# A new order of the instructions of one group in the semilinear stage, on TensorE, VectorE and ScalarE

## The reference, cut to what matters

```python
x = x + xattn(ctx, ctx, layernorm(x), ...)        # ends with "@ Wo.T + bo"
x = x + semilinear(layernorm(x), ...)             # the stage that changes
x = x + ffn(layernorm(x), gate_w, expert_w)       # expert = argmax of the scores

# semilinear: q, k, v = short_conv(h @ W), 4 taps along the tokens; lr = softplus(h @ Wlr + 0.001)
# the 32 tokens are 2 chunks of 16; per head (16 heads of 32) the state is W_in, W_out, 4 rows each
def step(carry, chunk):
    k_h = softmax(k . W_in) * lr;  q_h = softmax(q . W_in)
    qk = where(causal, q_h . k_h, 0)
    o = q_h @ W_out + qk @ v
    W_out = W_out + k_h.T @ v
    for _ in range(2):
        attn = softmax([W_in | W_out] . [k | v] * scale)     # over the tokens of the chunk
        G = attn @ [v | k]
        W_in, W_out = W_in + lr0 * G_in, W_out + lr1 * G_out
# output: o @ Wo, added to x
```

## Time and profile before

| | us |
|---|---|
| median of three runs | 1295.08 (1293.03 to 1295.43) |
| the profiled execution | 1292.32 |
| its span, first to last instruction | 1290.5 |
| TensorE busy in the span | 1073.4 (83%) |
| VectorE busy | 841.3 (65%) |
| ScalarE busy | 494.5 (38%) |
| GpSimd busy | 328.1 (25%) |
| first sk0 of group 0 | 533.95 |
| first sk0 of group 1, of group 7 | 599.66, 1047.99 |
| mean granted TensorE clock of the span | 0.905 of full |

### The profile page before, as it was taken

How to read it: one execution, slowest core, us unless ns; L and a number is a source line. 1 busy time by engine, 2 the same in 40 slices (tenths; PEclk the granted TensorE clock), 3 DMA queues, 4 the chain that set the end, 5 groups by cost and what they waited for, 6 DMA issues and landing times. The chain is left out here.

```text
span 1290.5 us, 18724 instructions
## 1 busy us (share of the span) xinstructions
PE 1073.4 (83%) x6268; PEld 795.1 (62%) x6268; DVE 841.3 (65%) x1611; ACT 494.5 (38%) x954; POOL 328.1 (25%) x297
## 2 busy tenths in 40 slices
PE   5993999999999836888898979888898966793997
PEld 4882656666666524676685857667585755673443
DVE  3664478778786843669687776968678694724332
ACT  1221366667775741334332423434242332420110
POOL 0345367757775620000000000000000000002453
PEclk9996989989999757989899989999899997775999
DMA  4372212102210002000101001010100020128441
GB/s 158 111 285 65 52 40 55 33 23 55 55 33 17 17 18 66 1 34 1 50 1 50 1 3 50 1 50 2 37 15 1 18 98 34 66 82 314 127 153 58
DMA packets 59925, 75.06 MB, mean 58 GB/s; under 512 B 37759, under 2 KB 42303, under 8 KB 57793
## 3 DMA queue, kind: packets, MB, share of 16 engines
q1 hardware_dynamic: 52384, 52.98, 13.0%
q0 software_dynamic: 5152, 12.59, 3.1%
q10 hardware_dynamic: 2304, 8.39, 1.6%
HBM read 56.65 MB, written 22.81 MB: 62 GB/s over the span
## 5 line engine op out<-in xcount | busy, mean ns | idle before, releaser
L1184 POOL COPY fw_hx<-fw_hT 128x128 f32<-128x128 f32 x32 | 8.0, 293 | 520.8 <-ACTq L1653 520.8
L544 POOL TENSOR_TENSOR aw_wtent<-aw_tent,aw_e 128x1760 f32<-128x1760 f32 x32 | 100.7, 3146 | 113.6 <-DVE aw_e L540 113.6
L733 PE MATMUL aw_psum_kv<-all_xWv,aw_c 128*128 128x512 f32 x256 | 124.4, 632 | 0.0
L516 POOL TENSOR_TENSOR aw_tent<-all_const,all_ix 128x1760 f32<-128x1760 f32 x32 | 100.6, 3146 | 5.1 <-POOL aw_wtent L544 4.6
L839 ACT ACTIVATE aw_cT<-aw_psum_av 32x256 f32<-32x256 f32 x128 | 80.6, 630 | 38.7 <-PE aw_psum_av L762 37.6
L721 PE MATMUL aw_psum_kv<-aw_c,all_xWk 128*128 128x352 f32 x256 | 81.2, 473 | 9.5 <-POOL aw_A L620 9.5
L1946 PE MATMUL ex_psum_y<-ex_We,ex_gT 128*128 x184 | 84.1, 602 | 0.0
L733 PEld LDWEIGHTS aw_psum_kv<-all_xWv,aw_c 128*128 128x128 f32 x256 | 49.2, 202 | 52.8 <-issue 51.0
L527 DVE TENSOR_TENSOR aw_prod<-aw_tent,aw_psum_s 128x1760 f32<-128x1760 f32 x32 | 63.5, 1984 | 23.3 <-ACT aw_tent L522 16.8
L1680 ACT ACTIVATE fw_at<-fw_at,fw_atop 128x128 f32<-128x128 f32 x128 | 49.5, 388 | 66.9 <-DVE fw_atop L1327 66.9
L743 PEld LDWEIGHTS aw_psum_s<-aw_K,aw_Qb 128*128 128x128 f32 x512 | 66.5, 208 | 6.8 <-issue 4.7
(11 more groups left out here) (258 smaller groups left out, 2251.4 us busy)
## 6 DMA issues: line engine op xcount, KB each, us to landing
ex_We<-expert SPq DMA_DIRECT2D x1, 8192.0 KB, 22.6
aw_craw<-ctx SPq DMA_DIRECT2D x8, 704.0 KB, 4.9
xh_scr<-fw_x SPq DMA_DIRECT2D x10, 512.0 KB, 3.7
pj_x<-x_tok SPq DMA_DIRECT2D x8, 512.0 KB, 3.9
q_scr<-pj_QT ACTq DMA_DIRECT2D x8, 512.0 KB, 2.9
aw_Qb<-q_scr SPq DMA_DIRECT2D x32, 128.0 KB, 3.5
c_scr<-aw_cT ACTq DMA_DIRECT2D x8, 512.0 KB, 2.7
fw_cT<-c_scr SPq DMA_DIRECT2D x8, 512.0 KB, 4.8
```

The costliest lines, as they stand in the source:

```text
L516: return nc.gpsimd.tensor_tensor(self.tent[r][:], bc(rows, 1, self.nu * NK), bc(ix, 2, self.wr), ALU.subtract)
L544: return eng.tensor_tensor(self.wtent[:], self.tent[r][:], bc(self.e[:].rearrange("p u k -> p (u k)"), 2, self.wr), ALU.mult)
L733: mm = nc.tensor.matmul(ps_kv[:, j % 2, :], rows, Wv[:, c, :], start=(c == 0), stop=(c == KC - 1))
```

## The change

The instructions of a group stay the same; their order changes on TensorE, VectorE and ScalarE, with both plans. TensorE's order per group becomes: y0 kt0 vt0 sk0 sq0 khT1 qhT1 y1 qk1 si0 o1 up z0 z1 so0 khT0 qhT0 t0 t1 qk0 q3 q1 q0 q2 ti0 to0 k0 gi0 vt1 go0 o0 si1 so1 k3 k1 lr v3 v2 ti1 v1 to1 gi1 go1 v0 k2 sk1 wo sq1. On VectorE the masks of qk1 stand ahead of the weights of chunk 0, `enter` is cut in two (`normal_rows` behind the update of W_out), the masks of qk0 stand behind the maxima of step 0, and convolutions stand singly or in pairs between the steps. On ScalarE the base copies stand in the same manner between the copies of ti, to, vt1, o0, and `rates_ln` behind the exponentials of chunk 1. `convolve` counts by the place in `CONV`, the plan's own order; `maxima` waits for both scores. The groups without a predecessor and the end are brought into the same order. Of the diff, the lines that are new or stay (those that go are in the functions above); indentation is cut:

```diff
+def normal_stats(nc, m, chain, x, stats, mv, var, tiles):
...
+def normal_rows(nc, chain, x, h, mv, rstd, std, tiles):
+
     chain.eng.wait_ge(std.sem, std.at(chain.i, 1))
     chain.link(nc.vector.reciprocal(rstd[:, 0:tiles], rstd[:, 0:tiles]))
...
+FRONT = [("y0", "dve"), ("y1", "dve"), ("t0", "act"), ("t1", "act"), ("q3", "dve"), ("q1", "dve"), ("q0", "dve"),
+         ("q2", "dve"), ("k0", "dve"), ("k3", "dve"), ("k1", "dve"), ("lr", "dve"), ("v3", "dve"), ("v2", "dve"),
+         ("v1", "dve"), ("v0", "dve"), ("k2", "dve")]
+CONV = [n for n, _ in FRONT if n[0] in "qkv"]
...
+BACK = [("kt0", "act"), ("vt0", "act"), ("sk0", "dve"), ("sq0", "dve"), ("khT1", "act"), ("qhT1", "act"),
+        ("qk10", "dve"), ("qk11", "dve"), ("qk12", "dve"), ("qk13", "dve"), ("si0", "dve"), ("o1", "act"),
+        ("up", "dve"), ("z0", "dve"), ("z1", "dve"), ("so0", "dve"), ("khT0", "act"), ("qhT0", "act"),
+        ("qk00", "dve"), ("qk01", "dve"), ("qk02", "dve"), ("qk03", "dve"), ("ti0", "act"), ("to0", "act"),
+        ("gi0", "dve"), ("vt1", "act"), ("go0", "dve"), ("o0", "act"), ("si1", "dve"), ("so1", "dve"),
+        ("ti1", "act"), ("to1", "act"), ("gi1", "dve"), ("go1", "dve"), ("sk1", "dve"), ("wo", "act"), ("sq1", "dve")]
...
# VectorE, group
     exponents(i, ch, 0)
     if has_prev:
         causal_products(i, 1)
     else:
+        back.skip_reads(dve, "dve", i, "qk10", "qk11", "qk12", "qk13")
+    dve.wait_ge(lr_done.sem, lr_done.at(i, 1))
+    weights(t, ch, 0)
+    masked(i, "si0", 0)
     if not last:
         enter(n)
+    add_own_heads(i, ch, "up", 0, wout0, wout).then_inc(w_done.sem, 1)
+    if not last:
+        entered(n)
     if has_prev:
         leave(t.prev(), i)
+    else:
+        back.skip_reads(dve, "dve", i, "z0", "z1")
     masked(i, "so0", 1)
     maxima(i, ch, 0)
     if last:
         gate_stats(0)
+    causal_products(i, 0)
     normalise(t, ch, 0)
+    ahead("q3", "q1", "q0")
     step_weights(i, ch, 0)
     if last:
         gate_rows(0)
+    ahead("q2")
     masked(i, "si1", 0)
+    ahead("k0")
     masked(i, "so1", 1)
     maxima(i, ch, 1)
+    if last:
+        gate_stats(1)
+    ahead("k3", "k1")
     if not last:
         rates_in(n)
     normalise(t, ch, 1)
+    ahead("v3")
     if not last:
         rates_add(n)
+    ahead("v2", "v1")
     step_weights(i, ch, 1)
     if last:
         gate_rows(1)
+    ahead("v0", "k2")
     exponents(i, ch, 1)
+    weights(t, ch, 1)
     if not last:
         rates_out(n)
     ch.close()
...
# TensorE, group
+    go("y0")
     pe.wait_ge(conv_done.sem, conv_done.at(i, 3 * KC))
+    transposes(i, back, "kt0", [key[:, g, halves[0]] for g in by_g])
+    transposes(i, back, "vt0", [v[:, g, halves[0]] for g in by_g])
     blocks(i, back, "sk0", KC, [(key[:, g, halves[0]], win0[:, g, :]) for g in by_g])
     blocks(i, back, "sq0", KC, [(q[:, g, halves[0]], win0[:, g, :]) for g in by_g])
+    if has_prev:
+        turned_softmax(t.prev(), i, 1)
+    else:
+        back.skip(pe, i, "khT1", "qhT1")
+    go("y1")
+    if has_prev:
+        causal(i, 1)
+    else:
+        back.skip(pe, i, "qk10", "qk11", "qk12", "qk13")
     blocks(i, back, "si0", KC, [(win0[:, g, :], key[:, g, halves[0]]) for g in by_g])
     if has_prev:
         output(t.prev(), i, 1)
     else:
+        back.skip(pe, i, "o1")
+    pe.wait_ge(p_done.sem, p_done.at(i, 1))
     pe.wait_ge(*back.used(i, "vt0"))
     blocks(i, back, "up", KC, [(vt[0][:, g, :], e[0][:, 0, g * P:(g + 1) * P]) for g in by_g])
+    if has_prev:
+        project(i, 0)
+        project(i, 1)
+    else:
+        back.skip(pe, i, "z0", "z1")
+    pe.wait_ge(w_done.sem, w_done.at(i, 1))
+    blocks(i, back, "so0", KC, [(wout[:, g, :], v[:, g, halves[0]]) for g in by_g])
+    turned_softmax(t, i, 0)
     go("t0", "t1")
     causal(i, 0)
+    go("q3", "q1", "q0", "q2")
+    pe.wait_ge(n_done.sem, n_done.at(i, 1))
+    transposes(i, back, "ti0", [at[:, 0, g, :] for g in by_g])
+    transposes(i, back, "to0", [at[:, 1, g, :] for g in by_g])
+    go("k0")
+    pe.wait_ge(*back.used(i, "ti0"))
+    blocks(i, back, "gi0", KC, [(vt[0][:, g, :], atT[:, 0, g, :]) for g in by_g])
+    transposes(i, back, "vt1", [v[:, g, halves[1]] for g in by_g])
+    pe.wait_ge(*back.used(i, "to0"))
+    blocks(i, back, "go0", KC, [(kt[:, g, :], atT[:, 1, g, :]) for g in by_g])
+    output(t, i, 0)
+    pe.wait_ge(w_done.sem, w_done.at(i, 2))
+    blocks(i, back, "si1", KC, [(win[:, g, :], key[:, g, halves[0]]) for g in by_g])
+    blocks(i, back, "so1", KC, [(wout[:, g, :], v[:, g, halves[0]]) for g in by_g])
+    if last:
+        gate_turn(0)
+        gate_score(0)
+        gate_turn(1)
+    go("k3", "k1", "lr", "v3", "v2")
+    pe.wait_ge(n_done.sem, n_done.at(i, 2))
+    transposes(i, back, "ti1", [at[:, 0, g, :] for g in by_g])
+    go("v1")
+    transposes(i, back, "to1", [at[:, 1, g, :] for g in by_g])
+    pe.wait_ge(*back.used(i, "ti1"))
+    blocks(i, back, "gi1", KC, [(vt[0][:, g, :], atT[:, 0, g, :]) for g in by_g])
+    pe.wait_ge(*back.used(i, "to1"))
+    blocks(i, back, "go1", KC, [(kt[:, g, :], atT[:, 1, g, :]) for g in by_g])
+    go("v0", "k2")
     if last:
         gate_score(1)
     pe.wait_ge(w_done.sem, w_done.at(i, 3))
     blocks(i, back, "sk1", KC, [(key[:, g, halves[1]], win[:, g, :]) for g in by_g])
+    transposes(i, back, "wo", [wout[:, g, :] for g in by_g])
     blocks(i, back, "sq1", KC, [(q[:, g, halves[1]], win[:, g, :]) for g in by_g])
...
# ScalarE, group
+    take(i, "kt0", kt[:])
     take(i, "vt0", vt[0][:])
+    if has_prev:
+        take(i, "khT1", khT[1][:])
+        take(i, "qhT1", qhT[1][:])
+    else:
+        back.skip_reads(act, "act", i, "khT1", "qhT1")
     exponentials(i, 0)
     if has_prev:
+        take(i, "o1", oT[:, :, P:2 * P])
     else:
+        back.skip_reads(act, "act", i, "o1")
+    if not last:
+        deviation(n)
     take(i, "khT0", khT[0][:])
     take(i, "qhT0", qhT[0][:])
     if not last:
         turned(n)
     row_exponentials(i, 0)
+    ahead("q3", "q1", "q0", "q2")
     take(i, "ti0", atT[:, 0])
+    ahead("k0")
     take(i, "to0", atT[:, 1])
     if last:
         gate_deviation(0)
+    take(i, "vt1", vt[1][:])
+    ahead("k3", "k1")
+    if last:
         gate_copy(0)
     row_exponentials(i, 1)
+    if last:
+        gate_copy(1)
     if not last:
         rates_exp(n)
+    ahead("v3")
+    take(i, "o0", oT[:, :, 0:P])
+    ahead("v2")
     take(i, "ti1", atT[:, 0])
+    ahead("v1")
     take(i, "to1", atT[:, 1])
+    if last:
+        gate_deviation(1)
+    ahead("v0", "k2")
+    take(i, "wo", wrow[:])
+    exponentials(i, 1)
     if not last:
         rates_ln(n)
```

More of the change, by code:

```diff
@@ L1145, in group @@
                 else:
-                    sp.wait_ge(*back.full(t.r, "sk0"))
+                    sp.wait_ge(*back.full(t.r, BACK[0][0]))
                     sp.wait_ge(x_out.sem, x_out.at(t.r - 1, 0))
@@ L1383, in group @@
                 exponents(i, ch, 0)
-                masked(i, "si0", 0)
-                dve.wait_ge(lr_done.sem, lr_done.at(i, 1))
-                weights(t, ch, 0)
                 if has_prev:
@@ L1420, in group @@
                     gate_rows(1)
-                ahead("v2", "v3")
+                ahead("v0", "k2")
                 exponents(i, ch, 1)
+                weights(t, ch, 1)
                 if not last:
                     rates_out(n)
-                weights(t, ch, 1)
                 ch.close()
             enter(FIRST)
-            convolve(FIRST, ["q0", "q1", "q2", "q3"])
+            entered(FIRST)
+            convolve(FIRST, CONV[:7])
             rates_in(FIRST)
             rates_add(FIRST)
-            convolve(FIRST, [f"{n}{e_}" for n in "kv" for e_ in range(KC)])
+            convolve(FIRST, CONV[7:])
             rates_out(FIRST)
@@ L1435, in _ @@
             rounds(dve, NG, group, 1)
-            back.skip_reads(dve, "dve", NG, *BEGIN)
+            back.skip_reads(dve, "dve", NG, "sk0", "sq0")
             gate_stats(2)
@@ L1439, in _ @@
             gate_rows(2)
+            back.skip_reads(dve, "dve", NG, "si0", "up")
             leave(LAST, NG)
@@ L1566, in group @@
-                transposes(i, back, "kt0", [key[:, g, halves[0]] for g in by_g])
-                go("y0", "y1")
+                if has_prev:
[7 more added lines that the diff above has]
+                    back.skip(pe, i, "qk10", "qk11", "qk12", "qk13")
                 blocks(i, back, "si0", KC, [(win0[:, g, :], key[:, g, halves[0]]) for g in by_g])
@@ L1611, in group @@
                 blocks(i, back, "sk1", KC, [(key[:, g, halves[1]], win[:, g, :]) for g in by_g])
+                transposes(i, back, "wo", [wout[:, g, :] for g in by_g])
                 blocks(i, back, "sq1", KC, [(q[:, g, halves[1]], win[:, g, :]) for g in by_g])
-                transposes(i, back, "vt1", [v[:, g, halves[1]] for g in by_g])
-                transposes(i, back, "wo", [wout[:, g, :] for g in by_g])
                 if last:
@@ L1623, in _ @@
             rounds(pe, NG, group, 1)
```

(20 more changed lines are left out.)

94 lines of the change are left out of this document (14 added, 80 removed), and 3 rows, old and new, of the table BACK.

## The result

The changed kernel takes 1239.8 us (median of four runs, 1232.5 to 1240.1) where the kernel before takes 1295.1 (1293.0 to 1295.4): ratio 0.956, 95% interval 0.953 to 0.960. Forecast: 1234, range 1220 to 1260. Run again on another occasion it took 1234.5 (1233.5 to 1237.5) against 1297.0, ratio 0.952 (0.950 to 0.953); this second base is the one for the experiments. These were run on three occasions, each with the kernel before beside it (1297.0, 1295.3 and 1296.5), so the ratios compare better than the medians.

What follows compares the result with a forecast made beforehand. TensorE, its waits and its slowed clock were taken to bound each 74.7 us group. Savings of 52.3 (six groups) + 4 + 5 = 61 from 1292.3 gave 1231, put at 1234 for the median; range 1220 to 1260.

Steps and rivals of the forecast that it cites:

- A group of 66.0 us: Groups 1 to 6 of the semilinear stage: each goes from 74.7 to 66.0 us, bounds 63.5 and 70.5.
- The replay: The new order worked through one steady group with profile durations: 64.7 us, 61.7 of work and 3.0 of waits.
- The branch, 0.85 on the mean: TensorE's wait at the loop's branch: adds 2.1 us in every second group, 0.45 filling an existing wait.
- The clock, 2.9 us per group: TensorE's o1 and following work, at the 1.2 GHz level behind a 2.67 us wait: 2.9 us lost per group.
- The table load: ScalarE's load of the exponential's table ahead of step 0, 1.28 us: covered by four q projections, priced at nothing.
- Group 0, 4 us: First group, with no chunk behind it: gain 4 us, bounds 0 and 6, with so0 waiting 5.7 us.
- Group 7, 5 us: Last group, without projections: kt0 to the step's transposes 37.9 us, step 0 saves another 1.6; gain 5, bounds 0 and 8.
- Behind it nothing changes: Claim that behind the last group, group 7, the time stays the same: no gain or loss.
- (a): Rival: waits come back in the steps behind base copies and convolutions; a group takes 70.5 to 71, total 1267; chance 0.12.
- (b): Rival: 63.5 to 64.5 us per group if the branch's wait falls into an existing one; 1222, down to 1216; chance 0.14.
- (c): Rival: TensorE's clock falls to 1.2 GHz during short pieces of work; a group takes 81 us, total 1330; chance 0.03.
- (d): Rival: VectorE's chain sets the 74.7 us group, so waits only move and nothing changes; 1295, chance 0.02.

Runs made afterwards that it cites:

- the weights first: Changed kernel with VectorE doing the softmax weights of chunk 0 ahead of the masks of chunk 1's causal products: 1258.0 us, ratio 0.969.
- matmuls of no use: Changed kernel with added 128x512 matmuls into a free PSUM bank where TensorE waits in the last group and gate's end: 1228.8 us, ratio 0.947.
- y1 in halves: Changed kernel with y1's eight matmuls issued in two halves, ahead of and behind the causal products of chunk 1: 1230.0 us, ratio 0.949.

## Why the prediction was right, point by point

**A group of 66.0 us: 66.46.** The replay gave 64.7 without the branch; the trace has 65.8, and without the loop 65.0. Its waits were 0.45, 0.9, 1.05, 0.3, 0.25; measured 0.65, 0.76, 0.78, 0.82, 0.24. Up's is the one that is far off: 0.82 in the loop, 0.40 without it, as VectorE has small pauses within the weights of chunk 0 that straight code lacks. The 0.45 added for hand-overs was too small by more than half for the 1.1 us that were missing, and its reason was mostly another: 0.8 of them go with the loop. The wait ahead of the turned softmax I had put down to the weights; the trace names the copy of vt0, which stands on ScalarE behind the logarithm's table load (601.85), moved there by the change. Both end within 0.1 us of each other (the weights at 604.33, the copy at 604.40), so taking one away alone would win 0.1 us at most. No run tries it.

**The branch, 0.85 on the mean: near, by luck.** I had a pause in every second group, three of six. The trace of the kernel before has two, which at the forecast's 1.65 us net would be 0.55 on the mean. In the changed kernel the two groups behind a branch take 3.1 and 1.6 us more than the other four, 0.8 on the mean, and 0.3 of that is a second cost that I missed, the fall of the clock behind one of the two (1.7 us). The kernel without a loop gains 1.5 us per group: this 0.8, and the 0.7 that every group has.

**The clock, 2.9 us per group: right in kind, the size is of group 1.** o1's first eight took 2.05 us in all six groups before and 1.13 after. TensorE's busy time in group 1 fell by 3.4 us, on the mean of the six before and the first five after by 2.4 (65.28 to 62.88, with the one fall behind a branch). With the weights first it fell again, in all six.

**The table load: right,** shown by moving it. The trace of the changed kernel has it at 1.28 us, and 1.40 from the end of ScalarE's last copy (627.20) to the first exponential (628.60). "ScalarE: Activation LUTs" of the Trainium skill (What ACT_TABLE_LOAD costs) adds a drain, 2.66 in all; the 1.40 us measured here have no room for one, and they decide.

**Group 0, 4 us: 3.6** (3.0 in the second profile). so0 waits 5.16 us there, forecast 5.7.

**Group 7, 5 us: 2.6. The step that failed is "Behind it nothing changes".** From sk1 of group 6 to the scores of step 0 it gained 6.3 us (45.07 to 38.78), where I had 3.4; from there to sk1 of group 7 it gained 1.4 (26.06 to 24.67), where I had 1.6; from there to the experts it lost 5.1 (49.00 to 54.09), where I had nothing. So two misses partly cancel. The work in the last stretch is the same, and so are its waits of 0.7 to 0.8 us ahead of the gate's scores. What differs is how long the matmuls take, at the lower clock level: 2.7 us of the loss lie ahead of the last z0 and z1 (a mean clock of 0.54, before 0.68), 2.4 behind them, where the last three sets of sixteen score matmuls take 3.58 us and before it was the last two, behind 1.85 and 1.95. With the matmuls of no use the last sets take 1.95, and this stretch 50.3; but they stand behind z0 and z1 only, and the part ahead of these stayed at 0.50. So for the second half an experiment shows that the clock is the cause, for the first half only the durations in the trace do; why the clock was lower there after the change is not shown.

**Sum.** 52.3 + 4 + 5 = 61 forecast; 49.5 + 3.6 + 2.6 = 55.7 measured. The median of the second occasion, 1234.5, lies on the forecast by luck: the base is 1.9 us higher there, and the stage in its profile is 55.0 us shorter, not 61. The rivals: (a) half a gain, did not happen, though the slack was as thin as said (0.2 us at go0, 0.4 at ti1, 1.7 at so0); (b), 63.5 to 64.5, was 2 to 3 us per group away and was reached by two more edits, y1 in halves and no loop; (c) did not happen, the clock is at 1.00 where it had 0.50; (d) fell.
